# Patch projection: fp32r passes over rounded parts and remainders for two of three chunks, with a smaller image ring

## What is computed

```python
patches = X.reshape(B, C, 8, 28, 8, 28).transpose(0, 2, 4, 1, 3, 5).reshape(B, 64, 2352)
tokens = einsum('bpi,hi->bph', patches, W) + b
h = concatenate([cls, tokens], 1) * pos_embed          # 65 tokens an image
h = h + attention(layernorm(h))   # 8 heads of 16; relu on q and k; scores over the sum of k; softmax
h = h + ffn(layernorm(h))         # shared SwiGLU + 8 experts in 2 groups, 2 experts a token, one expert input
```

## Time and profile before

| | us |
|---|---|
| median of 3 runs | 464.8 (464.34 to 466.05) |
| profiled execution, its own time | 468.48 |
| its span, first to last instruction | 466.7 |
| PE busy | 441.4 (95%) |
| DVE busy | 307.6 (66%) |
| ACT busy | 190.3 (41%) |
| POOL busy | 181.2 (39%) |
| mean granted clock of TensorE | 0.977 |

### The profile page before, as it was taken

How to read it: one execution, slowest core, us unless ns; L and a number is a source line. 1 busy time by engine, 2 the same in 40 slices (tenths; PEclk the granted TensorE clock), 3 DMA queues, 4 the chain that set the end, 5 groups by cost and what they waited for, 6 DMA issues and landing times.

```text
span 466.7 us, 6933 instructions
## 1 busy us (share of the span) xinstructions
PE 441.4 (95%) x2313; PEld 311.2 (67%) x2313; DVE 307.6 (66%) x896; ACT 190.3 (41%) x358; POOL 181.2 (39%) x220
## 2 busy tenths in 40 slices
PE   6969999899999999999999999999999999999982
PEld 2335455656786687667865788668856888887651
DVE  0151476486867876696659674868588877777665
ACT  1015523752276326641563238422752186321520
POOL 7112721222175306531652246304732256134453
PEclk9989999999999999999999999999999997899988
DMA  8998655135004520263007400530000000000000
GB/s 330 389 402 313 199 171 182 64 114 168 36 1 130 185 68 1 67 207 108 0 10 244 129 0 2 188 126 0 2 24 0 2 0 1 2 23 1 0 25 25
DMA packets 16451, 45.96 MB, mean 98 GB/s; under 512 B 1904, under 2 KB 7584, under 8 KB 16416
## 3 DMA queue, kind: packets, MB, share of 16 engines
q1 hardware_dynamic: 14704, 43.50, 27.8%
q10 hardware_dynamic: 1712, 2.02, 1.2%
HBM read 43.39 MB, written 2.13 MB: 98 GB/s over the span
## 4 chain that ended last, share of the span: by engine, by line
PE 77%; DVE 8%; DMA 4%; issue 4%; POOL 3%; ACT 2%; ACTq 1%; POOLq 0%; DVEq 0%
PE acc L483 22%; PE O L577 6%; PE B L469 6%; DMA bq_row<-in_bq_row 4%; PE scores L547 2%; PE scores L703 2%; PE C L703 2%; PE C L704 2%; PE C L705 2%; PE scores L705 2%; PE scores L704 2%; PE B L526 2%; PE C L635 2%; PE B L512 1%; PE C L665 1%
## 5 line engine op out<-in xcount | busy, mean ns | idle before, releaser
L483 PE MATMUL acc<-x_main,w_patch 128*128 128x512 f32 x288 | 141.4, 614 | 5.8 <-DMA w_patch<-in_w_patch 4.1
L483 PEld LDWEIGHTS acc<-x_main,w_patch 128*128 128x128 f32 x288 | 51.3, 195 | 48.3 <-issue 38.6
L1885 POOL TENSOR_TENSOR prod<-prod 128x512 f32<-128x512 f32 x31 | 39.9, 1286 | 27.9 <-DVE q_nat L1325 10.7
L993 ACT ACTIVATE probs_t<-B 128x512 f32<-128x512 f32 x32 | 19.1, 597 | 54.7 <-PE B L469 54.7
L577 PEld LDWEIGHTS O<-v_bd,probs_t 128*128 128x128 f32 x256 | 33.5, 200 | 10.4 <-issue 7.7
L1878 POOL TENSOR_TENSOR hidden_lo<-silu,hidden_hi 128x512 fp32r<-128x512 f32 x16 | 20.3, 1271 | 40.8 <-ACT hidden_hi L993 40.8
L577 PE MATMUL O<-v_bd,probs_t 128*128 128x64 f32 x256 | 33.2, 280 | 0.0
L1820 POOL TENSOR_TENSOR rstd<-var,neg_half 128x4 f32<-128x4 f32 x8 | 8.1, 1019 | 50.8 <-DVE var L1282 50.8
L1365 DVE TENSOR_TENSOR attn_patch<-O,row_rec 64x256 f32<-64x256 f32 x32 | 13.5, 422 | 21.5 <-PE O L577 20.8
L993 ACT ACTIVATE probs<-shift 128x512 f32<-128x512 f32 x32 | 20.1, 628 | 18.0 <-DVE shift L1338 16.8
L703 PE MATMUL scores<-w_eout_hi,hidden_hi 128*128 128x512 f32 x64 | 27.3, 426 | 0.0
(11 more groups left out here) (334 smaller groups left out, 1012.6 us busy)
## 6 DMA issues: line engine op xcount, KB each, us to landing
x_main<-in_x_main SPq DMA_DIRECT2D x40, 768.0 KB, 4.3
x_main<-in_x_main SPq DMA_DIRECT2D x8, 512.0 KB, 4.1
x_main<-in_x_main SPq DMA_DIRECT2D x8, 256.0 KB, 3.3
x_tail<-in_x_tail SPq DMA_DIRECT2D x8, 224.0 KB, 4.9
out_tokens<-y_out SPq DMA_DIRECT2D x14, 128.0 KB, 2.6
prod<-in_w_eout SPq DMA_DIRECT2D x2, 512.0 KB, 14.7
w_patch<-in_w_patch ACTq DMA_DIRECT2D x5, 192.0 KB, 10.1
silu<-in_w_in SPq DMA_DIRECT2D x2, 256.0 KB, 13.6
```

The lines of the kernel that those rows point to most:

```text
L483: last = mm(acc[:, :], w_patch[:, j, :], x_main[:, j, :], start=(j == 0), stop=False)
L993: return nc.scalar.activation(dst, src, func, **kw)
L1885: q.tensor_tensor(p[r, 0, :], p[r, 0, :], p[r, 1, :], ALU.add).then_inc(tree1_done.sem, 1)
```

## The change

For groups 3 to 7, chunks with j % 3 of 1 or 2 (12 of 18) are computed as three fp32r passes: rounded weights on rounded image, remainder weights on rounded image, rounded weights on image remainder. Chunks with j % 3 of 0, and groups 0 to 2, stay float32. The rounded weights `w_hi` and remainders `w_lo` are made in body 0 (two halves each, 128x768). All rounded images, the tails' too, go through four slots `x_hi`, `x_lo`: an "item" is a chunk or tail to be split, ACT rounds it (`item_high`), POOL subtracts (`item_low`), PE frees the slot (`chunk_used`, or `acc_full` for a tail). `split_high(pieces)` and `split_low(pieces)` issue the items up to four beyond those used by that many pieces. To make room, `x_main` becomes a ring of 9 chunks (piece loads wait for the chunk 9 before), `h_t` has one buffer, and small tensors are moved into others' space. The loads' loop is written out, with `store(g - 4)` between the third and fourth piece of group g. The fillers `FILLS` are as before.

```diff
+RING = 9
+SLOTS = 4
+FIRST_SPLIT = 3
+ITEMS = [(p, NMAIN) for p in range(FIRST_SPLIT)] + [(p, j) for p in range(FIRST_SPLIT, GROUPS) for j in range(NMAIN + 1)
+                                                    if j % 3 or j == NMAIN]
+def pieces_before(g, k):
+    return sum(sum(FILLS[b]) for b in range(1, g)) + sum(FILLS[g][:k])
+def items_ahead(pieces):
+    used = sum((p - FIRST_SPLIT) * (NMAIN + 1) + j < pieces for p, j in ITEMS)
+    return min(max(used, FIRST_SPLIT) + SLOTS, len(ITEMS))
...
+        w_hi = sb("w_hi", [128, NMAIN // 3, 2, D], F32R)
+        w_lo = sb("w_lo", [128, NMAIN // 3, 2, D], F32R)
-        x_main = sb("x_main", [128, NMAIN, TOK])
+        x_main = sb("x_main", [128, RING, TOK])
-        x_tail_hi = sb("x_tail_hi", [TAIL_ROWS, TOK], F32R)
-        x_tail_lo = sb("x_tail_lo", [TAIL_ROWS, TOK], F32R)
-        h_t = [sb(f"h_t{i}", [128, TOK]) for i in range(2)]
+        x_hi = sb("x_hi", [128, SLOTS, TOK], F32R)
+        x_lo = sb("x_lo", [128, SLOTS, TOK], F32R)
+        h_t = sb("h_t", [128, TOK])
...
@@ SP
             def load_piece(g, i, a, b):
-                    need(sp, x_used, g - 1, i + 1)
+                before = next(n for n, (_, end) in enumerate(PIECES) if end > (b - 1 - RING) % NMAIN)
+                need(sp, x_used, g if b > RING else g - 1, before + 1)
...
+            for g in range(4, GROUPS):
+                load_x(g, 0, 2)
+                load_tail(g)
+                load_x(g, 2, 3)
+                store(g - 4)
+                load_x(g, 3)
@@ PE, patch
+                    if (g, j) in ITEMS:
+                        n = ITEMS.index((g, j))
+                        hi, lo = item_sides(n)
+                        need(pe, xlo_done, n)
+                    if j == NMAIN:
+                        mm(acc[:, :], w_tail[:, :], hi, start=False, stop=False)
+                        mm(acc[:, :], w_tail[:, :], lo, start=False, stop=True).then_inc(acc_full.sem, 1)
+                    elif (g, j) in ITEMS:
+                        last = mm(acc[:, :], w_hi[split_chunk(j)], hi, start=False, stop=False)
+                        if ends:
+                            last.then_inc(x_used.sem, 1)
+                        mm(acc[:, :], w_lo[split_chunk(j)], hi, start=False, stop=False)
+                        mm(acc[:, :], w_hi[split_chunk(j)], lo, start=False, stop=False).then_inc(chunk_used.sem, 1)
@@ ACT, body and attention_filled
+                if is_int(g, 1):
+                    split_high(0)
                 load_table(g, 1, ACT.Exp)
                 exps(g, 0)
                 if last:
                     hidden_high(g - 1, 0, TOK)
+                    split_high(pieces_before(g, 1) + 2)
                 exps(g, 1)
...
                     route_exp(g - 1, TILES, 128)
+                    split_high(pieces_before(g, 2))
...
                 exps(g, 3)
+                if last:
+                    split_high(pieces_before(g, 4))
...
                     counts_out(g - 1, TOK)
+                    split_high(pieces_before(g, 7))
+                    split_high(pieces_before(g, 8))
                 natural(g + 1, 1 - par)
+                if not last:
+                    patch_weights_high(0)
...
                 attn_out(g)
+                if last:
+                    split_high(pieces_before(g, 9))
+                else:
+                    patch_weights_high(1)
                 normed_t(g + 1)
                 if last:
                     z_out(g, TOK)
+                else:
+                    item_high(3)
+                    item_high(4)
@@ DVE, tokens
                 need(dve, acc_full, g)
+                need(dve, nat_full, g - 1)
@@ POOL, body
                 bias_residual(g, par)
                 if last:
+                    if is_int(g, 1):
+                        split_low(0)
                     hidden_low(g - 1, 0, TOK)
+                    split_low(pieces_before(g, 1) + 2)
                     hidden_low(g - 1, 1, TOK)
+                    split_low(pieces_before(g, 2))
...
                 class_value(g, 0)
-                elif tail_ahead(g):
-                    tail_low(tail_ahead(g))
+                else:
+                    split_low(pieces_before(g, 4))
                 class_value(g, 1)
+                if last:
+                    split_low(pieces_before(g, 8))
                 norm_scale1(g + 1)
+                if last:
+                    split_low(pieces_before(g, 9))
                 norm_scale2(g, TILES, 128)
+                if not last:
+                    patch_weights_low(0)
+                    patch_weights_low(1)
+                    item_low(3)
+                    item_low(4)
                 need(pool, z_done, g)
```

More of the change, by code:

```diff
@@ L431, in _ @@
             load_x(0)
+            load_tail(0)
             load_piece(1, 0, *PIECES[0])
@@ L437, in _ @@
             load_x(1, 3)
+            load_tail(1)
             load_x(2)
[L439 to L444 removed]
+            load_tail(2)
+            load_x(3, 0, 2)
+            load_tail(3)
+            load_x(3, 2)
+            for g in range(4, GROUPS):
[4 more added lines that the diff above has]
+                load_x(g, 3)
+            for g in range(GROUPS - 4, GROUPS - 1):
                 store(g)
@@ L494, in to_natural @@
                 need(pe, sub_done, g - 1)
-                transposes(C1, [h_t[par][:, t * 128:(t + 1) * 128] for t in range(TILES)]).then_inc(nat_full.sem, 1)
+                transposes(C1, [h_t[:, t * 128:(t + 1) * 128] for t in range(TILES)]).then_inc(nat_full.sem, 1)
             def normed_t(g):
@@ L824, in fill_next @@
             def fill_next(g, k):
-                first = sum(sum(FILLS[b]) for b in range(1, g)) + sum(FILLS[g][:k])
-                for n in range(max(first, 1), first + sum(FILLS[g][k:k + 1])):
+                for n in range(max(pieces_before(g, k), 1), pieces_before(g, k + 1)):
                     p, j = divmod(n, NMAIN + 1)
@@ L1044, in exps, with split_high, item_high, patch_weights_high @@
                     .then_inc(exp_done.sem, 1)
-            def tail_high(g):
-                need(act, x_in[-1], g)
-                need(act, acc_full, g - 1)
-                go(x_tail_hi[:, :], x_tail[:, :]).then_inc(xthi_done.sem, 1)
+            rounded = [0]
+            def split_high(pieces):
+                for n in range(rounded[0], items_ahead(pieces)):
+                    item_high(n)
+                rounded[0] = items_ahead(pieces)
+            def item_high(n):
+                p, j = ITEMS[n]
+                need(act, x_in[-1 if j == NMAIN else next(i for i, (_, b) in enumerate(PIECES) if j < b)], p)
+                if n >= SLOTS:
+                    old, part = ITEMS[n - SLOTS]
+                    if part == NMAIN:
+                        need(act, acc_full, old)
+                    else:
+                        need(act, chunk_used, sum(i < NMAIN for _, i in ITEMS[:n - SLOTS]))
+                go(item_sides(n)[0], item_source(n)).then_inc(xhi_done.sem, 1)
+                rounded[0] = n + 1
+            def patch_weights_high(half):
+                raw, hi, _ = split_weights(half)
+                go(hi, raw).then_inc(wphi_done.sem, 1)
             def probs_out(g, p):
```

131 lines of the change are left out of this document (67 added, 64 removed).

## The result

The changed kernel takes 508.2 us (507.98 to 510.02 over four runs) against 464.6 (464.34 to 466.05): ratio 1.094, 95% interval 1.0906 to 1.0973. The forecast was 485, from 457 to 496. The direction was right and the size was not: 43.6 us were added where I had 20.8.

What follows compares the result with a forecast made beforehand. PE was taken to bound the kernel, with DVE close behind. 18.5 us for bodies 1 to 6 plus 2.3 between body 0 and 1, 20.8 on a median of 464.8, gave 485 us, range 457 to 496.

Steps and rivals of the forecast that it cites:

- Loads. I take 0: Ring loads land before PE needs them, and stores ahead of loads do no harm: 0, with 0 to 2 us for group 0.
- The sum's 18.5 us for bodies 1 to 6: DVE, stopped by POOL's remainders, holds PE: 3.4 us in each of bodies 1 to 5 and 1.5 in body 6.
- The term between body 0 and 1: POOL's weight remainders and two items run beside z_nat and ahead of z_low(0): cost 2.3 us, between 1 and 4.
- PE's gain, 0.17 us a chunk: Three fp32r passes take 0.69 us against 0.86 for a float32 chunk: 10.2 us less PE work over 60 chunks.
- ACT, "nothing": 60 more ACTIVATEs of 626 ns, with exps, probs_out and natural queued behind: cost nothing, at worst 0.6 us a body.
- POOL as supply: PE waits for the tail's remainder: 2.1 us in body 3, 1.6 to 2.1 in body 4; bounds 0 to 2.1 a body.
- DVE and POOL: POOL's remainders stop DVE's two-operand or scalar instructions 6 to 8 times a body; PE held 2.0 to 3.9 us, up to 4.8.
- the slack: Time that absorbs stops in a body: 2.77 us of DVE idle before attn_patch, 0.4 of holes, 0.5 of PE's lead.
- (c): Slower because POOL's remainders stop DVE, as summed: 485 us; chance 0.54.
- (a): Fewer than three stops a body, so PE's gain counts and the kernel is faster: 458 us; chance 0.20.
- (b): Fewer stops, but tail waits cost what the chunks save: no change, 465 us, 463 to 467; chance 0.14.
- (d): Slower by supply only: items come later than worked out, 2 us a body and no gain, 473 us; chance 0.12.

Runs made afterwards that it cites:

- three-moves run: The complete changed kernel with tail loads early, weights' roundings and remainders made at the start, and the store moved behind more loads: 494.7 us, ratio 1.0622.
- passes-store run: Changed kernel with early tail loads, ring of 12, no main-chunk pixel or weight remainders, store moved behind loads of chunks 3 to 11: 463.6 us, ratio 0.9936.
- split-free one with 18 chunks: Changed kernel with only tails split, tail loads early, and a ring of 18 chunks instead of 9: 468.1 us, ratio 1.0023.
- run of the passes: Changed kernel with early tail loads, ring of 12, no main-chunk pixel or weight remainders, store not moved: 471.4 us, ratio 1.0129.

## Why the forecast missed

Two steps of the prediction failed, by about the same amount. **"Loads. I take 0"** measured 10.6 us: the loads were compared with PE's use, and ACT reads them first. **The sum's 18.5 us for bodies 1 to 6** had the right mechanism, stops of DVE by POOL, and was too small by 10.5 us; it held no term for the clock, and had the late tokens of the next group only in its upper end. The term between body 0 and 1 was short by 1.9.

In ratios the 0.094 x 466 = 43.8 us split so: 7.8 tail loads, 4.2 weights' place, 2.8 store's place, 32.0 remainders on POOL (0.0686 x 466, of the three-moves run over the passes-store run), and −3.0 for the passes with their roundings. The forecast had 0 for the loads and the store (10.6), 2.3 for the weights' place (4.2) and 18.5 for the rest (29.0). By the intervals each part is uncertain by 2 to 4 us. The passes-store run also has a ring of 12 for nine: up to 4 us of the 32.0 can be the ring's.

- **PE's gain, 0.17 us a chunk:** right (0.23 us between passes; PE was busy for 434.2 us in the passes-store run and 443.6 in the split-free one with 18 chunks, at mean clocks of 0.973 and 0.974). But of 10.2 us only 4 to 8 reach the end even without remainders, and against the kernel before, with what the ring costs, 3. A shorter fill is worth nothing where the tail behind it waits (1.81 us in body 3), and part may have gone to the clock.
- **ACT, "nothing":** wrong, and not by the instructions' own time. I costed the ACTIVATEs and not what they wait for. ACT works in order and rounds ahead of PE, so a load that PE needs in ten microseconds is needed by ACT now: 9.76 us of wait in body 0 and 4.7 in body 2 stood ahead of `k_t` and the exponentials. The wait in body 0 is for a tail, which ACT rounded before the change too; the one in body 2 is for a chunk, and came with the new roundings.
- **Loads, "I take 0":** 7.8 + 2.8 us. I set the loads' times against PE's use; their first reader is ACT. And I named the stores in front of loads, then passed them over by the same comparison.
- **Between body 0 and 1, 2.3 us, from 1 to 4:** the mechanism was right, the size was not. `z_nat` alone lost 4.9 us, since four successive POOL instructions stopped four successive DVE ones; moving half of them gave 4.2 us back by the ratios, 3.1 in body 1.
- **POOL as supply, 2.1 us in body 3 and 1.6 to 2.1 in body 4:** right: 1.80 in body 3, and smaller in body 4 (1.11). The waits of the kernel after show the sum and its longest, 2.5 us in body 6, where I had none:

```profile
PE acc L520 <- POOL x_lo L1995: 6.0, 4, 2.5
...
PE acc L534 <- DVE h_t L1373: 4.8, 3, 2.7
```

- **DVE and POOL, 2.0 to 3.9 us a body, 3.4 taken:** right in place and mechanism, and in the number of stops. In bodies 1 to 6 of the kernel after 44 DVE instructions are lengthened by more than 0.3 us, 13, 9, 7, 4, 6 and 5 in turn, 44.4 us of excess in all (before 6, with 5.3); the forecast was 6 to 8 a body with 5.7 to 7.6 us. Body 3 grew by 3.5 us for 3.4. Bodies 4 and 5 grew by 4.8 and 4.9: that was the upper end, for tokens that come late, and the second row shows it (`h_t`, 2.7 us in body 4, 1.91 in body 5); up to 3.4 us of body 4's growth are half clock. Body 6 grew by 3.3 for 1.5, with the tail's 2.5 us in it. With the three orders mended bodies 1 to 6 are 26.1 us longer than before the change, where the sum had 18.5 and 2.3; up to 5.1 of them are half clock. The runs with POOL work that nobody waits for confirm both the stops and the slack.
- **The clock:** a term that the sum did not have, 8.0 us of PE's busy time and at most 10.5. In bodies 0 to 6 it comes with PE's gaps: in the kernel after, bodies 0, 1, 2, 4 and 6 have a gap of 5.24, 4.20, 3.47, 2.72 and 2.54 us and each a stretch at 1.2 GHz, bodies 3 and 5 have gaps of at most 1.91 and none. It doesn't follow every time: behind the 3.67 us of the run of the passes PE had its full clock (1.00 from 146.8 to 160.0 us, gap and all). Nor does it need a long gap: in the passes-store run it fell behind gaps of 1.11 and 1.81 us, and in the kernel before it was halved for 10.2 us from 390.7 on with no gap over 1 us in any body before it. What sets it is not settled here. It is not the main cause: in one run of the three-moves kernel the mean clock is 0.977 as before, and it is still 25 us longer than the profiled kernel before.

The page of the Trainium skill that I cited, "SBUF — State Buffer", section "Who interferes with whom", holds here in kind: a POOL instruction that reads SBUF stops DVE's two-operand forms, one that only writes does not, and PSUM readers go free. The scalar forms `g_sel` and `mv` were stopped by memsets too (0.61 us for 0.17), which my reading of the page in the prediction, readers of SBUF alone, did not cover. Of the four rivals the likeliest, (c), named the right mechanism, though 508 lies outside its range. (a) and (b) fall with the result. (d), supply alone, is excluded as the whole by the 35.0 us of subtractions that nobody waits for; as a part it stands, PE's waits for `x_lo` are 7.4 us in the kernel after. The range was too narrow because the sum held no bound for loads that an in-order engine reads ahead of PE, and none for the clock.

## What to carry to other kernels

When an engine is made to prepare data ahead of TensorE, check each load against that engine's turn, not TensorE's, and look at what stands ahead of the load in its queue: a store that waits 31 us is harmless until someone reads ahead. Before giving GpSimd more subtractions, count the short two-operand VectorE instructions beside them and VectorE's idle time in that stretch: up to that idle time they cost little (thirty cost 3.0 us by the medians and 8.8 by the bodies here), behind it each cost 0.7 to 0.9 us. A gain of a few per cent on TensorE is worth having only where nothing behind it waits for a neighbour; a new gap of some microseconds was followed by a stretch of half clock in most cases here, though not in all.

## What was not expected of the hardware

The stop doesn't depend on the size of what is stopped: `g_sel`, a TENSOR_SCALAR on 128x4 elements, went from 168 ns to 858 on average, 1.23 us beside a subtraction of 1.27. A run of DVE instructions can be stopped again by each next POOL instruction: `z_nat` needed 6.03 us for 1.11 beside four in a row. A memset of the same tile stops none of `comb` (366 ns) and `count`, but does stop the TENSOR_SCALARs `g_sel` and `mv`. PE's mean granted clock was 0.82 over the 5.7 us that hold the gap of 5.24 us, and 0.55 over the next 5.3, although PE was busy through all of these 5.3.
